# CIN tower, one core: new order of the first blocks' loads, copies and sums, and x_pairs rows padded to 42

## What is computed

```python
for i, (W, bias) in enumerate(params):                       # three layers, 200 outputs each
    x = jnp.einsum('bhd,bmd->bhmd', h, inputs).reshape(B, -1, D)
    y = jax.nn.relu(jnp.einsum('oi,bid->bod', W, x) + bias[None, :, None])
    if i != n_layers - 1:
        h, direct = jnp.split(y, 2, axis=1)                  # 100 maps go on, 100 are results
    else:
        direct = y
    outs.append(direct)
z = jnp.concatenate(outs, axis=1).sum(-1)
h = jnp.maximum(jnp.concatenate([z, dense_ctx], axis=1) @ W_top1 + b_top1, 0.0)
h = jnp.maximum(h @ W_top2 + b_top2, 0.0)
y = h @ W_top3
```

## Time and profile before

| | us |
|---|---|
| median of 3 runs | 2821.92 |
| lowest, highest | 2819.53, 2822.87 |
| profiled execution | 2822.93 |
| its span, first to last instruction | 2821.1 |

### The profile page before, as it was taken

One profiled execution on the slowest core, in us unless ns is written; L12 is line 12 of the kernel. 1 busy time (PEld: TensorE's weight loads), 2 busy tenths in 40 slices (PEclk: granted clock), 3 DMA queues, 4 the chain that ended last, 5 costly groups with the idle time before them and its releaser, 6 DMA issues.

```text
span 2821.1 us, 54038 instructions
## 1 busy us (share of the span) xinstructions
PE 2775.4 (98%) x19012; PEld 2758.2 (98%) x19012; DVE 2637.9 (94%) x1945; ACT 1500.6 (53%) x1880; POOL 858.7 (30%) x700
## 2 busy tenths in 40 slices
PE   5999999999999999999999999999999999999999
PEld 4999999999999999999999999999999999999997
DVE  6999999999999999999999999999999999999995
ACT  4555555555555555555555555555555555555553
POOL 5433332332332332332323323323323323333100
PEclk9999999999999999999999999999999999999999
DMA  7333333433433433333334334334333334334330
GB/s 210 85 83 84 86 94 78 94 87 76 99 88 75 100 84 82 97 84 85 93 79 94 87 78 97 89 75 102 85 78 99 85 82 95 85 86 94 85 78 18
DMA packets 286025, 249.66 MB, mean 89 GB/s; under 512 B 31286, under 2 KB 284446, under 8 KB 285893
## 3 DMA queue, kind: packets, MB, share of 16 engines
q1 hardware_dynamic: 216310, 200.56, 25.4%
q0 software_dynamic: 65712, 45.56, 12.1%
q10 hardware_dynamic: 3972, 3.17, 0.4%
HBM read 140.74 MB, written 4.20 MB: 51 GB/s over the span
## 4 chain that ended last, share of the span: by engine, by line
PE 94%; POOL 2%; DVE 1%; DMA 1%; issue 1%; SPq 0%; ACT 0%; another core or an unknown queue 0%; DVEq 0%; ACTq 0%; POOLq 0%
PE acc L809 62%; PE acc L811 29%; POOL gathered L445 1%; PE z_ps L826 1%; PE hid_ps L822 1%; DVE tails L721 1%; DMA acc_copy<-acc_copy 1%; DVE product L716 1%; PE acc L880 0%; SPq L380 0%; DMA gathered<-in_table,rows_all 0%; PE hid_ps L903 0%; DMA hid_rep<-hid 0%; ACT acc_copy L528 0%
## 5 line engine op out<-in xcount | busy, mean ns | idle before, releaser
L809 PE MATMUL acc<-weights,heads 126*128 126x400 f32 (+1 forms) x9088 | 2694.1, 364 | 16.3 <-DVE tails L721 16.2
L811 PE MATMUL acc<-weights,tails 126*128 126x200 f32 (+1 forms) x9088 | 2321.6, 255 | 0.0
L522 ACT ACTIVATE heads<-product 126x1024 fp32r<-126x1024 f32 (+2 forms) x1152 | 1198.1, 1047 | 1021.5 <-PE acc L811 507.3
L811 PEld LDWEIGHTS acc<-weights,tails 126*128 126x128 f32 (+1 forms) x9088 | 1740.8, 192 | 0.0
L809 PEld LDWEIGHTS acc<-weights,heads 126*128 126x128 f32 (+1 forms) x9088 | 1712.9, 188 | 19.7 <-issue 10.0
L721 DVE TENSOR_TENSOR tails<-product,heads 126x1024 fp32r<-126x1024 f32 (+2 forms) x1152 | 1348.9, 1204 | 1.4 <-ACT heads L522 1.1
L716 DVE TENSOR_TENSOR product<-hid_rep,x_rep 126x2048 f32<-126x2048 f32 x510 | 1167.4, 2289 | 96.5 <-PE acc L811 64.8
L453 POOL DMA_DIRECT2D acc_copy<-acc_copy x189 | 235.0, 1244 | 1719.8 <-ACT acc_copy L528 1716.4
L445 POOL DMA_INDIRECT gathered<-in_table,rows_all x320 | 510.8, 1596 | 101.4 <-issue 97.1
L536 ACT ACTIVATE y_relu<-acc_copy 128x400 f32<-128x400 f32 x192 | 102.4, 533 | 217.0 <-DMA acc_copy<-acc_copy 215.0
L528 ACT ACTIVATE acc_copy<-acc 128x800 f32<-128x800 f32 x192 | 158.7, 827 | 9.8 <-PE acc L811 7.7
(11 more groups left out here) (26 smaller groups left out, 118.2 us busy)
## 6 DMA issues: line engine op xcount, KB each, us to landing
x_rep<-x_rows SPq DMA_DIRECT2D x512, 120.0 KB
hid_rep<-hid SPq DMA_DIRECT2D x511, 120.0 KB
x_pairs<-x_rows SPq DMA_DIRECT2D x191, 280.0 KB
acc_copy<-acc_copy POOLq DMA_DIRECT2D x189, 200.0 KB
hid_rep<-hid SPq DMA_DIRECT2D x511, 5.0 KB
x_pairs<-x_rows SPq DMA_DIRECT2D x63, 120.0 KB
gathered<-in_table,rows_all POOLq DMA_INDIRECT x320
raw_weights<-in_w SPq DMA_DIRECT2D x8, 500.0 KB, 6.1
```

The lines of the kernel that those rows point to most:

```text
L522: act.activation(heads[0:rows, ring % HEADS_RING, 0:tiles, :], product[0:rows, ring % PRODUCT_RING, 0:tiles, :], ACT.Copy).then_inc(heads_ ...
L809: nc.tensor.matmul(acc[:, at.parity, c, 0:2 * LAYER], dims(heads[0:rows, ring % HEADS_RING, k, :], c), w, start=(q == 0 and k == 0), stop= ...
L811: last = nc.tensor.matmul(acc[:, at.parity, c, LAYER:2 * LAYER], dims(tails[0:rows, ring % PRODUCT_RING, k, :], c), w[:, 0:LAYER], start=F ...
```

## The change

Five things are changed, four of them in the steps before the loop.

1. **Rows.** `x_pairs` gets 42 rows a shift in place of 40, 126 partitions in place of 120; the bias row of layer 0 moves to partition 126. The two further rows are fields again, and their weights are zero.
2. **Step 0 on SP.** The second half of block 0's `x_rep` is issued behind the maps of block 0 and not ahead of them.
3. **Step 1 on SP.** Of the seven chunks of `w2`, three are loaded where all were, and four behind the maps of block 1.
4. **Step 1 on ScalarE.** `copy_acc` of slot 1 stands behind two heads of layer 1 and not behind four, and its `relu` ahead of the seventh head, not behind it.
5. **GpSimd.** For blocks 4 and 5 all three sums stand ahead of the five gathers. Before, one sum stood ahead of them, and for block 5 one gather ahead of that sum. From block 6 on the order is as it was.

```diff
@@ -47,6 +47,8 @@
 SHIFTS = 3
 TILES0 = (FIELDS // 2 + 1) // SHIFTS
 PAIRS0 = SHIFTS * FIELDS
+FIELDS_PADDED = 42
+ROWS0 = SHIFTS * FIELDS_PADDED
 
 REPEATED = -(-(SHIFTS * TILES0 - 1) // FLD_PART)
 ROWS_X = FIELDS + REPEATED * FLD_PART
@@ -64,7 +66,7 @@
 GROUPS0 = 2
 TILE_BASE = (0, TILES0, TILES0 + TILES)
 ALL_TILES = TILES0 + 2 * TILES
-OPERAND_ROWS = (PAIRS0 + 1, PAIRS + 1, PAIRS + 1)
+OPERAND_ROWS = (ROWS0 + 1, PAIRS + 1, PAIRS + 1)
 
 PRODUCT_RING, HEADS_RING = 6, 4
 RING = 12
@@ -313,13 +315,13 @@
 
         def pairs_parts(duo, parity):
 
-            parts = [(x_pairs[0:PAIRS0, 0, :],
-                      block_rows(duo, parity, 0, FIELDS).unsqueeze(1).to_broadcast([FIELDS, SHIFTS, COLS]))]
+            parts = [(x_pairs[0:ROWS0, 0, :],
+                      block_rows(duo, parity, 0, FIELDS_PADDED).unsqueeze(1).to_broadcast([FIELDS_PADDED, SHIFTS, COLS]))]
             for j in range(SHIFTS):
-                rows = block_rows(duo, parity, j, FIELDS)
-                parts.append((x_pairs[j:PAIRS0:SHIFTS, 1:1 + TILES0, :],
+                rows = block_rows(duo, parity, j, FIELDS_PADDED)
+                parts.append((x_pairs[j:ROWS0:SHIFTS, 1:1 + TILES0, :],
                               bass.AP(tensor=rows.tensor, offset=rows.offset,
-                                      ap=[[COLS, FIELDS], [SHIFTS * COLS, TILES0], [1, COLS]])))
+                                      ap=[[COLS, FIELDS_PADDED], [SHIFTS * COLS, TILES0], [1, COLS]])))
             return parts
 
         @block.sync
@@ -336,7 +338,7 @@
             for dst, src in ((ident[:, :], ident_in), (sum16[:, :], sum16_in), (z_t[HALF:HALF + DENSE, 0, :], dense_t),
                              (wt3_sb[:, :], wt3), (bt1_sb[:, :], bt1), (bt2_sb[:, :], bt2)):
                 sp.dma_start(dst, src).then_inc(consts_loaded, 16)
-            for row in (x_pairs[PAIRS0:PAIRS0 + 1, :, :].rearrange("p a c -> p (a c)"),
+            for row in (x_pairs[ROWS0:ROWS0 + 1, :, :].rearrange("p a c -> p (a c)"),
                         x_rep[PAIRS:PAIRS + 1, :, :, :].rearrange("p a b c -> p (a b c)")):
                 sp.dma_start(row, ones_in[:, 0:row.shape[1]]).then_inc(ones_loaded, 16)
 
@@ -397,12 +399,11 @@
                     load_pairs(duo, 1 + parity)
                 if not whole and i == 0:
                     load_x_rep(0, 0, 0)
-                    load_x_rep(0, 0, 1)
                 if not whole and 0 < i < blocks and l2 is None:
 
                     for half in range(FLD_HALVES):
                         load_x_rep(duo, parity, half)
-                    load_weights(split_until[1], split_until[2])
+                    load_weights(split_until[1], split_until[1] + 3)
                 if whole or i < blocks:
 
                     if not whole:
@@ -410,6 +411,10 @@
                     if l1 is not None:
                         sp.wait_ge(products_made, l1.group + GROUPS)
                     load_hid(0, (0, 2, 3) if not whole and i == 0 else range(HID_OUT))
+                    if not whole and i == 0:
+                        load_x_rep(0, 0, 1)
+                    if not whole and i == 1:
+                        load_weights(split_until[1] + 3, split_until[2])
                     for half in range(FLD_HALVES) if l2 is not None else ():
 
                         sp.wait_ge(products_made, l2.group + (half + 1) * HID_OUT)
@@ -472,15 +477,14 @@
 
             for b in range(FIRST, blocks):
                 first = 1 + (b - FIRST) * 3
-                ahead = 1 if b == FIRST + 1 else 0
-                for k in range(ahead):
-                    gather(0, k, rows_all[:, b, k:k + 1], x_gathered)
-                add(first)
-                for k in range(ahead, FLD_DMA):
+                sums_ahead = 3 if b < FIRST + 2 else 1
+                for n in range(sums_ahead):
+                    add(first + n)
+                for k in range(FLD_DMA):
                     gather(0, k, rows_all[:, b, k:k + 1], x_gathered)
                 pool.wait_ge(x_gathered, (b - (FIRST - 1)) * GATHERS)
-                add(first + 1)
-                add(first + 2)
+                for n in range(sums_ahead, 3):
+                    add(first + n)
                 for part in stored_parts(b, 0):
                     pool.dma_start(*part).then_inc(x_stored, 16)
                 pool.wait_ge(x_stored, (b - (FIRST - 1)) * STORES)
@@ -602,6 +606,8 @@
                 split_heads(*split_now(0))
                 for q in range(2) if first else ():
                     make_heads(*first, q)
+                if odd is None and i == 1:
+                    copy_acc(*l0)
                 if before:
                     copy_acc(*before)
                 split_heads(*split_now(2))
@@ -609,7 +615,7 @@
                     make_heads(*first, q)
                 if before:
                     relu(*before)
-                if l0 and first:
+                if l0 and first and not (odd is None and i == 1):
                     copy_acc(*l0)
                 split_heads(*split_now(4))
                 for q in range(4, 6) if first else ():
@@ -618,9 +624,11 @@
                     copy_turned(*before)
                     before = None
                 split_heads(*split_now(6))
+                if odd is None and i == 1:
+                    relu(*l0)
                 if first:
                     make_heads(*first, 6)
-                if l0 and first:
+                if l0 and first and not (odd is None and i == 1):
                     relu(*l0)
                 if first:
                     make_heads(*first, 7)
@@ -923,7 +931,7 @@
     w0a = np.zeros((128, TILES0, LAYER), w.dtype)
     w0b = np.zeros((128, TILES0, LAYER), w.dtype)
     w0a[:PAIRS0] = w[:, i, m].transpose(2, 1, 3, 0).reshape(PAIRS0, TILES0, LAYER)
-    w0a[PAIRS0, 0] = arr("L0_rec_b0")
+    w0a[ROWS0, 0] = arr("L0_rec_b0")
     w0b[:PAIRS0] = w[:, m, i].transpose(2, 1, 3, 0).reshape(PAIRS0, TILES0, LAYER)
     w0b[0:PAIRS0:SHIFTS, 0] = 0
     w0b[SHIFTS - 1:PAIRS0:SHIFTS, TILES0 - 1] = 0
```

## The result

The changed kernel takes 2829.05 us in the median of 18 runs (2819.88 to 2831.93), the kernel before 2821.38 us in 18 runs on the same chips (2816.78 to 2824.05). The ratio is 1.0025 with a 95% interval of 1.0018 to 1.0031: slower by 0.25%, some 7 us. The forecast was 2837.6. The profiled execution took 2830.74 us, so its sum is told against the profiled execution of the kernel before, 2822.93 us: +7.8 us.

The account below looks back on a forecast made before the run. VectorE was taken as the bound from 64 to 116 us, TensorE in the middle. Terms -1.0 + 0.95 - 1.94 + 15.9 + 1.8 = +15.7 us on 2821.9 gave 2837.6 us, range 2819 to 2841.

Parts of the forecast that it names:

- Maps of block 0: VectorE's start at 45.32: maps ahead of x_rep's second half gain between 0 and 2.29 us, taken as 1.0.
- Copy ahead: Block 1's first copy ahead of two heads: ends VectorE's 2.52 us wait at 63.70, priced 0 for TensorE.
- four chunks behind: w2 chunks behind block 1's maps: one is split at 76.65, VectorE took it at 75.70, +0.95 us.
- Waits before 133.33 and 136.67: TensorE's two idle times before later tails vanish as block 5's second sum precedes its gathers: -1.94 us.
- The held gathers: Block 4: four gathers held until VectorE stops, slot 4's sum late, TensorE waits from 111.01: +15.9 us; chance 0.58.
- The rival with "a last gather between 98.9 and 110": Block 4's last gather ends then; stall between 0 and 11 us, say 2828 us; chance 0.08.
- Landing 3.39, stores 4.24, sum 3.60: Times in us after block 4's gathers: their landing, two stores with landing, then slot 4's sum.
- Clock, +1.8: After the stop at slot 4's turn TensorE's clock is 0.91 over 20 us: +1.8 us.
- Block 5's gathers, 0: Behind its third sum they end their chain at 151.8, 2.6 us late; taken as 0, up to 1.
- The free pace: Five gathers unheld by VectorE take 9.7 us; for block 4 a rival, 2819.9 us, sharing chance 0.24.
- Rows of 42: Block 0's first x_pairs load carries 5% more bytes, covered by VectorE's wait at 45.32: cost 0.
- The rival by one instruction of VectorE: Each block 4 gather waits for at most one VectorE instruction: 2826 us, or 2819.9 with half; shares chance 0.24.

Follow-up runs that it names:

- e8: The kernel of e7 with four of w2's seven chunks ahead of block 1's maps and three behind: 2816.13 us, ratio 0.9983.
- e2: The kernel before with only the changed GpSimd queue: 2834.99 us, ratio 1.0044.
- e12: The kernel of e8 with x_rep's second half ahead of block 0's maps again: 2815.58 us, ratio 0.9985.
- e7: The changed kernel with GpSimd's queue of before, but all five gathers of block 5 ahead of its first sum: 2816.92 us, ratio 1.0.
- e11: The kernel of e8 with slot 1's copy and ReLU where they were before: 2814.44 us, ratio 0.9979.
- e1: The changed kernel with GpSimd's queue of before: 2820.2 us, ratio 0.9997.
- e10: The kernel of e8 with 40 rows a shift again: 2816.49 us, ratio 0.9989.
- e4: The changed kernel with three sums ahead of the gathers for block 5 only, one for block 4: 2822.77 us, ratio 1.0003.
- e5: The changed kernel with a one-element VectorE memset ahead of each pair of tails in steps 2 and 3: 2817.2 us, ratio 0.999.
- e6: The changed kernel with a 4 KB store to DRAM between block 4's second and third gather: 2828.93 us, ratio 1.0027.
- e9: The kernel of e5 with four of w2's chunks ahead of block 1's maps and three behind: 2816.59 us, ratio 0.9986.

## Why the prediction came out as it did

The direction was right, and the place of one wait: TensorE waits at the turn of slot 4 because the sum stands behind held gathers. The size was not: +15.7 us forecast, +7.8 measured in the profile.

- **Maps of block 0, -1.0.** VectorE started at 44.53, 0.79 us sooner than at 45.32. The size fits, but e8, which has the edit too, starts at 42.95, and e2 and e12, which haven't, at 43.82 and 43.47: the starts of two executions differ by more than the edit is worth, and it is not shown to be the cause.
- **Copy ahead, 0, and four chunks behind, +0.95.** The fold at 60.31 no longer waits (before 2.52), and the fourth chunk made VectorE wait 1.78 us, where I had 0.95. Taken together VectorE needs 78.93 - 44.53 = 34.40 us from its start to TensorE's restart, before 35.05: -0.65 where the two terms gave +0.95. I had priced the fold's wait at 0 though VectorE was the bound there, in my own reading. In the medians neither shows: e8 against e7 is 0.8 us for the chunk, e11 is not slower than e8 for the copy.
- **Waits before 133.33 and 136.67, -1.94.** Right: both are gone, and e1, with the sums undone, has them again, 0.61 and 0.73 us, together 1.34.
- **The held gathers, +15.9. This is the step that failed.** "The first gather gets through by 94.3": it ended at 92.88. "The four others are held, as the one at 105.51 was, until VectorE stops": they are not. The last ended at 102.03, not at 114.8, and the wait is 2.33 us. I had two held gathers in one stretch before my eyes and made of them a state that lasts; but each stood alone behind other work of GpSimd, and neither had a second gather close behind it inside the stretch. The trace of before showed the rest, and I had not set it beside VectorE's stretch: block 4's gathers there (GpSimd's timeline, rows below). The first was held until VectorE's stop, 57.17 + 4.96 - 0.94 = 61.19; the last two run at 1.79 and 1.97 us inside the stretch without a gap that begins at 63.70. The rival with "a last gather between 98.9 and 110" had 0.08 and is what happened to block 4: by its scale 102.0 gives a wait of 3.1.

```profile
57.17 4.96 POOL L445 DMA_INDIRECT gathered<-in_table,rows_all  x1 [0.30 <-issue]
...
64.99 1.79 POOL L445 DMA_INDIRECT gathered<-in_table,rows_all  x1 [0.30 <-issue]
67.09 1.97 POOL L445 DMA_INDIRECT gathered<-in_table,rows_all  x1 [0.30 <-issue]
```

- **Landing 3.39, stores 4.24, sum 3.60:** measured 1.98, 3.44 and 111.74 - 107.68 = 4.06.
- **Clock, +1.8:** 1.23 by the marks behind the first wait; the window shows 0.91, as forecast.
- **Block 5's gathers, 0. The second failed step.** "From 134.2 they need 9.7 + 3.39 + 4.24 + 0.3": the five took 132.91 to 153.13, 20.2 us, because I held the gathers of block 4 and let those of block 5 go free, behind the same three sums. Its price is 6.45 + 1.73 us and it is the larger part of the loss. The free pace would have been right: at 151.8 the sum would have been in time, since a turn at 163.48 - 6.45 = 157.03 needs it by 152.9 (its way to the turn is 163.48 - 159.37 = 4.11).
- **Rows of 42, 0.** Nothing to be seen (e10).
- **The rival by one instruction of VectorE.** Its conflict is borne out, its length is not where time was lost. 7.35 us of holding at 84.59 (8.29 less 0.94) span seven instructions of VectorE. Block 4's first gather in e1, e4, e7 and e8 did get in behind the one that ran. The Trainium skill (SBUF — State Buffer, Who interferes with whom) gives the port that the two engines share to the one who came first for its whole instruction; the traces agree in that held gathers start where an instruction of VectorE ends, and disagree that it is always the next one. The Trainium skill (same page and section) also says that a VectorE instruction with at most one SBUF input, outside the modes that use two ports, doesn't contend; e5's memset, which has none, took the long holds away, in agreement.

The times of 2826 for that rival and 2828 for the late gathers lie nearer to the result than the main case, but not by their own reckoning: both had the whole loss at block 4, where it was 2.33 + 1.23 us, and nothing at block 5, where it was 6.45 + 1.73.

**What stays open.** At which boundary of VectorE's instructions a first gather is let in, and why the later ones pass at ordinary boundaries; e6 excludes only that a DMA of another kind between gathers matters. The traces give a hint that nobody tested. Up to 330 us, in the kernels without memsets, a first gather that got in ahead of a stop did so where the semaphore for VectorE's next instruction had come late: 0.10 us before the running one ended (93.32 in the kernel before), 0.15 us before (e1, e4, e7, e8, e10 and e12 at 52 to 55 us), or just at its end (e8 at 88.43, e12 at 88.95). Where one was passed over, that semaphore had been there for 0.20 us or more, or the instruction waited for none. There is one exception each way: e6 at 83.55, passed over with 0.15 us, and e11 at 56.54, let in with 1.44. Open is also why the runs of the changed kernel spread from 2819.88 to 2831.93, those of e5 only from 2815.86 to 2819.26: the length of a hold hangs on how VectorE runs beside it, and that could differ between executions, but only one execution of each was profiled.

## What to carry to other kernels

Where a queue that feeds the critical path also issues indirect gathers, ask for each first gather of a row where the next stop of VectorE lies, take the wait up to there as the upper bound, since a gather can be let in sooner, and price it the same way for every block that gets the same order, not only for the first. An outlier in the minimum, median and maximum of a line tells that there are holds; whether they take one gather or all five must be read from the neighbours of the long one. Where the order has to stay, an instruction of 0.06 us without inputs in VectorE's queue, ahead of each pair of tails, took the long holds away here and cost nothing that could be measured.

## What the hardware showed that was not expected

- The first gather of a row of them, issued into a stretch of VectorE without a stop, can be held over seven and more instructions, up to 11.12 us with its own 0.94. It starts within 0.05 us of the end of an instruction of VectorE: at the stop in the four long holds at 105.51, 84.59, 132.91 and (e4) 131.22, without a stop at 93.32 in the kernel before and at 88.43 in e8.
- Direct DMAs of the same queue are not held: the sum at 84.52, inside the stretch of 52.00 us, took 1.20 us.
- A memset of one element, 0.06 us, between instructions of two inputs does what a stop does: no gather of blocks 4 to 6 in e5 and e9 takes more than 2.66 us. It does not shift them: product at 86.20 and tails at 88.41 in e5, 86.70 and 88.91 in the changed kernel, 2.21 us apart in both.
